# Moving one expert pair in eight from VectorE to ScalarE, and adding whole pairs on GpSimd, in an attention and mixture-of-experts block

## The reference, cut to what matters

```python
q = moe_proj(q_proj); k = moe_proj(k_proj); v = moe_proj(v_proj)   # each (n, 128)
scores = jnp.einsum('bth,bsh->bts', q, k) / sqrt(h)
attn = softmax(scores, axis=-1)                    # over all 4096 tokens
o = jnp.einsum('bts,bsh->bth', attn, v)
z = jnp.einsum('ne,nh->enh', w, o)                 # w: weights of the 16 experts
out = jnp.einsum('enh,ehc->nc', z, o_proj)         # sum over experts, (n, 256)
```

## Time and profile before

| what | value |
|---|---|
| median of 3 runs | 1484.52 us (1482.84 to 1484.77) |
| profiled execution, own time | 1481.75 us |
| its span, first to last instruction | 1480.0 us |
| around the span | 1.75 us |
| mean granted TensorE clock | 0.967 |
| busy: PE, DVE, POOL, ACT | 1394.3, 1146.8, 716.1, 679.6 us |
| block 5 (steps 0 to 31) | 1222.10 to 1299.11 us |
| block 7 up to the sum matmuls | 1374.86 to 1447.22 us |

### The profile page before, as it was taken

How to read it: one execution, slowest core, us unless ns; L and a number is a source line. 1 busy time by engine, 2 the same in 40 slices (tenths; PEclk the granted TensorE clock), 3 DMA queues, 4 the chain that set the end, 5 groups by cost and what they waited for, 6 DMA issues and landing times. The chain is left out here.

```text
span 1480.0 us, 23971 instructions
## 1 busy us (share of the span) xinstructions
PE 1394.3 (94%) x6880; PEld 1215.9 (82%) x6880; DVE 1146.8 (77%) x2185; ACT 679.6 (46%) x1345; POOL 716.1 (48%) x633
## 2 busy tenths in 40 slices
PE   5669999999999999999999799999998999999997
PEld 3458899999998999999999777878786878778775
DVE  5758586776767767766667598989897999999865
ACT  3340220303103022130101198887887788888983
POOL 3231131301313013130014077889887888989897
PEclk8688999999999999999999899999999999999998
DMA  4230010010100111000226420000001000000000
GB/s 135 70 96 17 29 38 27 28 38 29 39 27 26 39 30 38 27 26 24 62 84 217 143 112 16 15 29 15 30 8 39 9 15 30 16 30 15 15 16 21
DMA packets 84698, 63.55 MB, mean 43 GB/s; under 512 B 15520, under 2 KB 77392, under 8 KB 84304
## 3 DMA queue, kind: packets, MB, share of 16 engines
q1 hardware_dynamic: 56656, 46.69, 10.0%
q10 hardware_dynamic: 27904, 15.21, 3.5%
HBM read 36.72 MB, written 25.17 MB: 42 GB/s over the span
## 5 line engine op out<-in xcount | busy, mean ns | idle before, releaser
L1425 PE MATMUL ps<-w_hi,memory_r 128*128 128x384 f32 x2048 | 569.1, 343 | 6.1 <-DVE w_lo L858 2.6
L1217 DVE SCALAR_TENSOR_TENSOR wst<-ps,w_cur,wst 128x384 f32<-128x384 f32 x480 | 295.7, 616 | 178.1 <-PE ps L1425 170.7
L1425 PEld LDWEIGHTS ps<-w_hi,memory_r 128*128 128x128 f32 x2048 | 377.0, 190 | 10.6 <-DVE w_lo L858 2.7
L1643 POOL TENSOR_TENSOR memory_rest<-memory_rest,pf 128x512 f32<-128x512 f32 x248 | 348.7, 1406 | 69.8 <-ACT pf L1745 63.7
L1425 PE MATMUL ps<-w_lo,memory_r 128*128 128x384 f32 x1024 | 345.1, 337 | 0.0
L1810 DVE TENSOR_TENSOR p_lo<-pf,p_hi 128x512 fp32r<-128x512 f32 x256 | 280.6, 1096 | 44.5 <-ACT p_hi L1747 38.8
L1425 PEld LDWEIGHTS ps<-w_lo,memory_r 128*128 128x128 f32 x1024 | 194.3, 190 | 4.8 <-issue 1.4
L1745 ACT ACTIVATE pf<-ps 128x512 f32<-128x512 f32 x256 | 153.5, 600 | 81.5 <-PE ps L1917 64.9
L1705 ACT COPY ps<-shift_rows 128x512 f32<-128x512 f32 x256 | 152.7, 597 | 6.5
L1747 ACT ACTIVATE p_hi<-ps 128x512 fp32r<-128x512 f32 x256 | 152.1, 594 | 0.0
L1792 DVE TENSOR_REDUCE mx<-ps 128x1 f32<-128x512 f32 x224 | 147.6, 679 | 0.4 <-PE ps L1908 0.4
(11 more groups left out here) (213 smaller groups left out, 2116.5 us busy)
## 6 DMA issues: line engine op xcount, KB each, us to landing
qk_scratch<-wst ACTq DMA_DIRECT2D x56, 128.0 KB, 2.2
memory<-in_x SPq DMA_DIRECT2D x8, 512.0 KB, 4.2
x_scratch<-memory SPq DMA_DIRECT2D x8, 512.0 KB, 3.1
o_scratch<-memory_rest SPq DMA_DIRECT2D x16, 256.0 KB, 3.1
x2b<-x_scratch SPq DMA_DIRECT2D x32, 128.0 KB, 2.1
out_x<-memory_rest SPq DMA_DIRECT2D x32, 128.0 KB, 1.7
v_scratch<-wst ACTq DMA_DIRECT2D x60, 64.0 KB, 1.7
memory_r<-qk_scratch SPq DMA_DIRECT2D x9, 256.0 KB, 4.7
```

What stands on the lines that cost most here:

```text
L1217: nc.vector.scalar_tensor_tensor(out=dst, in0=src, scalar=w, in1=dst, op0=ALU.mult, op1=ALU.add).then_inc(moe_acc, 1)
L1425: ins = nc.tensor.matmul(ps[:, s % MOE_BANKS, 0:H3], x_part[p][:, k, rows], w_part[:, k, e].rearrange("p t h -> p (t h)"), start=(k == 0 a ...
L1643: nc.gpsimd.tensor_tensor(p_sum[:, p], p_sum[:, p], pf[:, j % PB], ALU.add).then_inc(p_summed, 1)
```

## The change

`MAIN` becomes `Split((0, 2, 4, 6))`: ScalarE scales four pairs of eight, every second one, and VectorE the other four. ScalarE's ring `act_half` gets four buffers in place of three. GpSimd waits for two scaled pairs and adds them as whole pairs of 512 columns, adds the third and the fourth in the same way, and then once a tile folds the two halves of the sum into one (256 columns). `act_total` moves to a tensor of its own.

```diff
-        act_half = sb("act_half", [P, PB, 2, C])
+        HALVES = 4
+        act_half = sb("act_half", [P, HALVES, 2, C])
...
+        act_total = sb("act_total", [P, 2, 2 * C])
...
-        MAIN, TAIL = Split((1, 4, 6)), Split((0, 2, 4, 6))
+        MAIN, TAIL = Split((0, 2, 4, 6)), Split((0, 2, 4, 6))
+        FOLDS = MAIN.act_per_tile
...
-                    first = j % PAIRS == MAIN.act_pairs[0]
-                    done = upto(i, p, TT * MAIN.adds, t * MAIN.adds + 2 * (m - t * MAIN.act_per_tile) - (not first))
-                    halves = [act_half[:, m % PB, n] for n in range(2)]
+                    of = m - t * MAIN.act_per_tile
+                    done = upto(i, p, TT * FOLDS, t * FOLDS + of - 1)
                     total = act_total[:, t % 2]
+                    scaled = [act_half[:, n % HALVES].rearrange("p a c -> p (a c)") for n in (m - 1, m)]
+                    if of == 0:
+                        return
                     pool.wait_ge(act_scaled, upto(i, p, MAIN.act_per_block, m + 1))
-                    if first:
+                    if of == 1:
                         wait(pool, yo_ready, upto(i, p, TT, t - 1))
-                        nc.gpsimd.tensor_tensor(total, halves[0], halves[1], ALU.add).then_inc(act_summed, 1)
+                        nc.gpsimd.tensor_tensor(total, scaled[0], scaled[1], ALU.add).then_inc(act_summed, 1)
                     else:
-                        for n in range(2):
-                            pool.wait_ge(act_summed, done + n)
-                            nc.gpsimd.tensor_tensor(total, total, halves[n], ALU.add).then_inc(act_summed, 1)
+                        pool.wait_ge(act_summed, done)
+                        nc.gpsimd.tensor_tensor(total, total, scaled[1], ALU.add).then_inc(act_summed, 1)
+                    if of == MAIN.act_per_tile - 1:
+                        pool.wait_ge(act_summed, done + 1)
+                        nc.gpsimd.tensor_tensor(total[:, 0:C], total[:, 0:C], total[:, C:2 * C], ALU.add
+                                                ).then_inc(act_summed, 1)
```

More of the change, by code:

```diff
@@ L1479, in adaln_block_kernel @@
         shift_rows = sb("shift_rows", [P, BT])
-        act_half = sb("act_half", [P, PB, 2, C])
+        HALVES = 4
+        act_half = sb("act_half", [P, HALVES, 2, C])
         w_out_s = sb("w_out_s", [P, 2, TT, E])
-        y, yo, act_total = (rest[:, 2 * BT + n * 2 * C:2 * BT + (n + 1) * 2 * C].rearrange("p (a c) -> p a c", a=2)
-                            for n in range(3))
+        act_total = sb("act_total", [P, 2, 2 * C])
+        y, yo = (rest[:, 2 * BT + n * 2 * C:2 * BT + (n + 1) * 2 * C].rearrange("p (a c) -> p a c", a=2)
+                 for n in range(2))
         x2b = sb("x2b", [P, TT, C])
@@ L1713, in scale_half @@
                     act.wait_ge(o_mm, upto(i, p, NT, j + 1))
-                    held = m - PB
+                    held = m - HALVES
                     tile, of = divmod(held, MAIN.act_per_tile)
-                    wait(act, act_summed, upto(i, p, TT * MAIN.adds, tile * MAIN.adds + 2 * of + 1))
+                    wait(act, act_summed, upto(i, p, TT * FOLDS, tile * FOLDS + max(of, 1)))
                     for n in range(2):
                         e = 2 * pair + n
-                        ins = nc.scalar.mul(act_half[:, m % PB, n], ps[:, Y_BANK + j % 2, n * C:(n + 1) * C],
+                        ins = nc.scalar.mul(act_half[:, m % HALVES, n], ps[:, Y_BANK + j % 2, n * C:(n + 1) * C],
                                             w_out_s[:, p, t, e:e + 1])
```

4 lines of the change are left out of this document (2 added, 2 removed).

## The result

| | kernel before | changed kernel |
|---|---|---|
| median of 21 runs each | 1484.09 us (1480.03 to 1486.17) | 1488.08 us (1482.78 to 1497.98) |
| ratio, 95% interval | | 1.0033 (1.0021 to 1.0045) |
| profiled execution, its span, clock | 1481.75, 1480.0, 0.967 | 1484.13, 1481.9, 0.968 |

The account below looks back on a forecast made before the run. TensorE paces the middle of blocks with VectorE also at its limit, and GpSimd bounds block 7. Terms -3.7 + 2.6 - 0.7 = -1.8 us gave 1482.7 us, with an 8-in-10 range of 1479 to 1488.

Parts of the forecast that it names:

- steps 4 to 18 stay at 35.1 us: Middle of a block: TensorE sets the pace with 155 matmuls, so this stretch would not change.
- VectorE's relief: Steps 19 to 27, six blocks: one pair in eight fewer on VectorE returns 3.7 of 4.4 us lost; bounds 4.4 and 0.
- a mean p_lo that rises by 0.07 us: Steps 4 to 27: p_lo waits longer behind GpSimd, 0.49 us in place of 0.42, costing VectorE 1.7 us.
- The slower rival: Steps 19 to 27 and block ends: p_lo waits behind longer additions, VectorE stays at its limit; +4.1 us, 1488.6 us, chance 0.2.
- a mean above 1.23 us: Middle of a block: mean p_lo at which VectorE's 1.1 us of room in 24 steps would be used up.
- My formula: p_lo's mean wait: half the sum of squares of GpSimd's instruction times over the time; 0.42 us before, 0.49 after.
- Block 7: GpSimd is the bound there; pair additions and folds lengthen its list by 3.3 us, term +2.6 us, bounds +1.0 and +3.5.
- the faster rival: Block 7 costs next to nothing more and VectorE's relief is whole; -4.9 us, 1479.6 us, chance 0.25.
- what p_lo takes from GpSimd stays the same: Block 7: GpSimd's time lost to p_lo was taken as unchanged, since the number of p_lo is unchanged.
- The end of the blocks: Six block ends: last softmax addition 0.25 us earlier, -1.5 us, against a possible +1.5 from step 28's addition; taken as -0.7.
- cost 0: ScalarE's two extra instructions in 8 steps, 0.96 us, stay hidden under TensorE's step.
- The clock rival: Block 7: more idle TensorE time brings one more half-clock stretch, about 4 us; +2.2 us, 1486.7 us, chance 0.1.

Follow-up runs that it names:

- e6: Changed kernel with GpSimd's pair additions cut from 512 to 8 columns in blocks 2 to 6 alone (wrong sums there): 1486.32 us, ratio 1.0018.
- the second execution: The changed kernel unaltered, run and profiled once more: 1488.60 us over 12 runs, ratio 1.0025; the profiled execution took 1494.35 us.
- e4: Changed kernel with each 512-column pair addition issued as two of 256 columns: 1494.92 us, ratio 1.0073.
- e3: Changed kernel with the old three pairs (1, 4, 6) on ScalarE, so only whole-pair additions and the fold are new: 1477.13 us, ratio 0.9953.
- e2: Kernel before with the new split (0, 2, 4, 6) and the fourth buffer, but additions in halves as before: 1498.44 us, ratio 1.0094.
- e12: Changed kernel with ScalarE's scaling cut to 8 columns of each half in blocks 2 to 7 (wrong sums): 1488.79 us, ratio 1.0022.
- e7: Changed kernel with GpSimd's pair additions cut to 8 columns in blocks 2 to 7 (wrong sums there): 1474.60 us, ratio 0.9924.
- e11: e7 with ScalarE's scaling also cut to 8 columns of each half in blocks 2 to 7 (wrong sums): 1469.72 us, ratio 0.9895.
- e10: Changed kernel with pairs 1, 3, 5 and 7 on ScalarE in place of 0, 2, 4 and 6: 1487.37 us, ratio 1.0018.
- e8: e7 with the three old pairs (1, 4, 6) on ScalarE (wrong sums): 1471.30 us, ratio 0.9916.
- e9: e3 with only pairs 4 and 6 of each tile on ScalarE and GpSimd in block 7, VectorE taking six; computation complete: 1472.54 us, ratio 0.992.

## Why the prediction was wrong

**The step that failed** is "steps 4 to 18 stay at 35.1 us", together with the term of VectorE's relief, -3.7 us, which counted steps 19 to 27 alone. The relief came there (-3.6 and -2.8 us in the two executions). But steps 4 to 18 lost +2.9 and +3.8 us, so the middle of the blocks as a whole gave -0.7 and +1.0. e6 shows the cause, GpSimd's pair additions: with these cut to 8 columns the stretch is back at 210.92 us.

**Why I didn't see it.** I worked with averages over 24 steps: VectorE's work 55.1 us against TensorE's 56.2 (busy times, which hold waits as well as work), and a mean p_lo that rises by 0.07 us. Over blocks 1 to 6 the mean hardly moved, 1116 ns. But that hides two halves: in steps 4 to 18 it rose from 1123 to 1187 ns (1218 in the second execution), and in steps 19 to 27 it fell from 1102 to 986 (1035). And a search matmul waits on one reduction, and that one waits behind the p_lo before it. With three GpSimd instructions of 512 columns in a row, two p_lo in a short time each lasted 1.7 to 1.8 us (block 3, steps 13 to 15), and 1 us of TensorE was gone, though VectorE caught up later. The slower rival named the right mechanism (p_lo behind longer additions) and the wrong place, steps 19 to 27, and its test, a mean above 1.23 us, couldn't have caught this. The rival's number, 1488.6 us, is half a us from the measured one by luck: most of the 4.4 us did come back in steps 19 to 27, and the block ends gained time and didn't cost it. e4 adds that two additions of half the length gave the same loss; what the length and the amount of GpSimd's work each do isn't separated.

**Which half brings the relief.** The prediction put it down to the pair taken from VectorE. e3 had all of it with the three old pairs, and e2 had none of it with four. VectorE's time is as much a matter of GpSimd's list as of its own. My formula, a p_lo that comes at no particular moment, doesn't hold here. Worked for e2 (sixteen additions in 18.74 us, eight of 1.26 and eight of 0.72) and for e3 (ten of 1.26 and two of 0.72), it gives the same wait for both, 0.45 us, a little more than its 0.42 for the kernel before. The measured waits in steps 4 to 27 are 0.56 us in e2, 0.41 in e3 and 0.44 before. So it can't tell the two apart by which VectorE gained or lost.

**Block 7**: the mechanism was right (chain on GpSimd, additions of 512 columns), and the term was mis-sized: +3.75 us in both executions, against +2.6. The bare difference of 3.3 us was sound, but I took 0.7 us off it for waits between additions and at the block's start, and counted the waits for p_lo as unchanged. They grew: the means are 1.62 us for a pair addition of 1.26 and 1.18 us for a fold of 0.72, together (12 x 0.36) + (3 x 0.46) = 5.7 us, against (15 x 0.25) + (4 x 0.33) = 5.1 before. By the faster rival this should have fallen, since there are fewer instructions; it is refuted. That what p_lo takes from GpSimd stays the same, as the prediction had it, is wrong too. The Trainium skill (GPSIMD Engine Reference, 3.1) gives 4497 ns for an addition of 2048 columns, by which 512 columns are an estimated 1.12 us and 256 0.56. The trace has 1.26 and 0.72. From the one to the other that is 2.13 ns a column, near the page's 2.20, and it leaves 0.17 us for each instruction whatever its width, which is what whole pairs save.

**The end of the blocks**: -2.8 and -1.9 us in steps 28 to 31, against -0.7. The shape that I gave (the softmax addition starts 0.25 us earlier, and so the last p_lo waits that much less) is what e3 has in all blocks of the loop: p_lo 1.41 to 1.43 us in place of 1.68 to 1.69. (2.00 - 1.7 is 0.3, where the prediction used 0.25.) In the changed kernel only block 3 has it. In blocks 2, 4 and 5, and in 4 and 5 of the second execution, the gain is some 0.75 us each and comes in another way, which the prediction hadn't: the order of the two turned, and the last p_lo is ahead of the softmax addition and not behind it.

**ScalarE, "cost 0"**: wrong by a little. Step 30 took 2.58 us in place of 2.38 in blocks 2 to 5, and step 1 2.6 to 2.7 us in blocks 3 to 5 (the timeline above has the wait there, 1.04 us for ScalarE's copy of the shift). In the changed kernel this doesn't set the time (e12); in e7 it probably does (e11 is 4.9 us faster, with overlapping intervals).

**The clock rival** expected one more stretch at half clock in block 7. There the stretch was as before. The extra ones are at block starts: 9 of the 10 profiled executions with four pairs had at least one besides the back edge's (e10 had none), and of the four with three pairs (before, e3, e8, e9) none had. Each 3.4 us stretch costs TensorE an estimated 1.7 us. In the changed kernel one of them follows the wait of 1.06 us in step 1 of block 3, TensorE's timeline:

```profile
1065.53 0.50 PE L1923 MATMUL ps<-memory_r 128*128 128x512 f32 x1 [1.06 <-ACT ps L1713]
...
1067.08 0.63 PE L1979 MATMUL ps<-o_hi,ot_lo 128*128 128x512 f32 x1
```

That this wait is the cause is not shown: block 5 has a wait of 1.04 us at the same place and no such stretch, and the stretches stayed when ScalarE's scaling was cut (e11, e12). With 14 profiled executions that they go with the fourth pair is likely; why, and why e10 has none, stays open.

**The sum.** Forecast -1.8 us, measured +4.0. Against the forecast the two profiles have +2.9 and +3.8 us in steps 4 to 18, +0.1 and +0.9 in steps 19 to 27, +1.2 in block 7, +0.2 and +6.1 at the block starts (the clock and ScalarE), -2.1 and -1.2 at the block ends, and -0.6 and -0.5 in the tail. That is 1.7 us for the one and 10.3 for the other. The 5.8 us between forecast and measurement lie between them, and some 0.7 of it outside the span. No term of the sum had a cost for the block starts; the clock's rival looked for it in block 7.

## What to carry to other kernels

When work moves from one engine to another over a shared port, look at the third engine's list too: here the version that moves nothing and only makes GpSimd's list shorter (e3) gained 7 us, and the pair moved away from the loaded VectorE cost 11. Of these, 5.6 are block 7, where GpSimd's list is the bound, and 2 to 3 are steps 4 to 18, where VectorE and GpSimd wait for each other. Where a stretch is at the pace of TensorE but the engine beside it has under 2% of idle time (34.47 of 35.13 us), don't book it as "stays": count single waits there, not means. And an edit can be right in the middle of a program and wrong in its last block; the split that suits each (e9) beat both kernels, 1472.5 us against 1484.1 and 1488.1.
